# Self-attention transposes copied a step later, and cross-attention steps that begin with the scores

## The reference, cut to what matters

```
# part 1: causal self-attention, 16 heads of 32, gated
proj = layer_norm(x) @ W_in.T + b_in                 # q, k, v, p, y
k = (1 - smear) * k + smear * k_prev
pos = cumsum(sigmoid(y))                             # forget gates
attn = softmax(q k^T / sqrt(32) + causal - relpos)
x = LN(x + LN(silu(p) * (attn @ v) @ W_out.T))
# part 2: cross-attention, 16 heads of 64: queries from x, keys and values
# from 512 rows (256 of the context, masked, and the 256 of x itself)
q = LN(x) @ Wq ; k, v = concat(LN(ctx), LN(x)) @ Wkv
x = LN(x + softmax(q k^T / 8 + mask) v @ Wout)
# part 3: mixture of 8 experts, top 2, width 1024
x = LN(x + sum over the two experts of gate * (gelu(x W1 + b1) W2 + b2))
```

## Time and profile before

| | |
|---|---|
| runs, median | 2735.02 us |
| profiled execution | 2734.17 us, span of its instructions 2732.4 us |
| PE busy | 2407.9 us (88% of the span) |
| DVE, ACT, POOL busy | 1824.2, 1730.1, 924.7 us (67, 63, 34%) |
| mean granted TensorE clock | 0.954 of full speed |

### The profile page before, as it was taken

How to read it: one execution, slowest core, us unless ns; L and a number is a source line. 1 busy time by engine, 2 the same in 40 slices (tenths; PEclk the granted TensorE clock), 3 DMA queues, 4 the chain that set the end, 5 groups by cost and what they waited for, 6 DMA issues and landing times. The chain is left out here.

```text
span 2732.4 us, 60996 instructions
## 1 busy us (share of the span) xinstructions
PE 2407.9 (88%) x17862; PEld 1991.3 (73%) x17862; DVE 1824.2 (67%) x5239; ACT 1730.1 (63%) x4346; POOL 924.7 (34%) x983
## 2 busy tenths in 40 slices
PE   4888888888499999999999999999999469999991
PEld 3666666666377777777777777777776369999991
DVE  5666666667466667666676667666675268888876
ACT  4777787777356566666666666665665256666762
POOL 2434434443423332233322332223321124444434
PEclk9999999999699999999999999999999679999995
DMA  5545445445100000000000000000000157777765
GB/s 122 154 108 123 104 100 123 106 99 118 40 17 17 9 9 16 16 16 1 16 16 16 9 8 16 16 16 9 9 16 9 46 193 232 231 239 234 242 223 192
DMA packets 160229, 224.40 MB, mean 82 GB/s; under 512 B 33872, under 2 KB 127696, under 8 KB 159568
## 3 DMA queue, kind: packets, MB, share of 16 engines
q1 hardware_dynamic: 149040, 201.88, 26.5%
q0 software_dynamic: 9664, 20.53, 2.2%
q10 hardware_dynamic: 1376, 0.54, 0.1%
HBM read 140.15 MB, written 24.01 MB: 60 GB/s over the span
## 5 line engine op out<-in xcount | busy, mean ns | idle before, releaser
L1514 DVE CUSTOM_DVE_ANT_0 x_prob<-x_score,x_mask_add 128x512 f32<-128x512 f32 x512 | 347.9, 682 | 286.7 <-PE x_score L1745 232.0
L1317 ACT ACTIVATE x_prob<-x_prob,x_low 128x512 f32<-128x512 f32 x512 | 366.4, 718 | 190.3 <-DVE x_low L1514 188.0
L1323 ACT COPY x_pt<-x_ptb 128x512 f32<-128x512 f32 x512 | 272.9, 584 | 255.3 <-PE x_ptb L1757 254.7
L1238 POOL TENSOR_TENSOR x_k_lo<-x_whole,x_k_hi 128x512 fp32r<-128x512 f32 x128 | 168.0, 1313 | 413.6 <-ACT x_k_hi L1363 411.2
L1757 PE MATMUL x_ptb<-ident,x_prob 128*128 128x128 f32 x2048 | 267.4, 274 | 2.0 <-PEq L1788 1.8
L1525 DVE TENSOR_SCALAR x_prob<-x_prob,x_rden 128x512 f32<-128x512 f32 x512 | 264.7, 558 | 0.6
L1774 PE MATMUL x_av<-x_pt,x_vx 128*64 128x256 f32 x2048 | 251.0, 387 | 0.8 <-ACT x_pt L1323 0.8
L1757 PEld LDWEIGHTS x_ptb<-ident,x_prob 128*128 128x128 f32 x2048 | 230.4, 141 | 13.8 <-issue 11.1
L484 ACT ACTIVATE prob<-prob,low 128x128 f32<-128x128 f32 (+1 forms) x512 | 229.9, 457 | 5.0 <-DVE low L727 4.8
L1494 DVE COPY x_whole<-x_proj 128x512 f32<-128x512 f32 x192 | 131.0, 688 | 141.7 <-PE x_proj L1678 140.2
L490 ACT COPY pt<-ptb 128x384 f32<-128x384 f32 x258 | 122.4, 474 | 140.5 <-PE ptb L895 140.5
(11 more groups left out here) (274 smaller groups left out, 7283.9 us busy)
## 6 DMA issues: line engine op xcount, KB each, us to landing
w_s<-w SPq DMA_DIRECT2D x156, 512.0 KB, 4.8
k_parts<-k_hi SPq DMA_DIRECT2D x128, 128.0 KB, 2.4
q_parts<-q_hi SPq DMA_DIRECT2D x128, 128.0 KB, 2.4
k_parts<-pos_parts SPq DMA_DIRECT2D x128, 64.0 KB, 2.4
k_parts<-k_lo SPq DMA_DIRECT2D x64, 128.0 KB, 2.4
q_parts<-q_lo SPq DMA_DIRECT2D x64, 128.0 KB, 2.3
w_s<-expert_rows SPq DMA_DIRECT2D x16, 512.0 KB, 4.8
b_s<-b SPq DMA_DIRECT2D x39, 128.0 KB
```

Source lines behind the costliest of these rows:

```text
L1238: pool.tensor_tensor(part_of(n, q_lo, k_lo), whole_of(n), part_of(n, q_hi, k_hi).bitcast(F32), ALU.subtract).then_inc(low_ready.sem, 1)
L1317: nc.scalar.activation(slot, slot, ACT.Exp, bias=low[:, u:u + 1], scale=-1.0, accum_out=den[:, u:u + 1]).then_inc(exp_ready.sem, 1)
L1323: nc.scalar.copy(pt[:, u % PX_RING, :], ptb[u % 2][:, :]).then_inc(pt_taken[u % 2].sem, 1)
L1514: dve.tensor_tensor_reduce(prob[:, u % PROB_RING, :], score[u % 2][:, :], mask_add[:, :], -X_SCALE, 3.0e38, ALU.add, ALU.min, low[:, u:u + ...
```

## The change

In the self-attention a second constant `COPY_LAG = 3` stands beside `LAG = 2`. ScalarE copies the transposes of head i - 3 in step i instead of those of head i - 2, and does so after the parts of the step instead of before them; TensorE still makes the transposes of head i - 2 in step i, and computes the values of a group a step later (steps 3, 7, 11 and 15 instead of 2, 6, 10 and 14). Three dummy transposes are made once before the loop, so that the first copies have something to read.

In the cross-attention TensorE's step begins with the scores of step i + 1, then come the split products, the transposes of step i - 2, the values, and the whole parts. The scores of the next element's first step move from step 17 to step 18. The ring of probabilities has 8 slots instead of 6. ScalarE and VectorE take the projected parts a step later, and some value parts too.

```diff
--- before.py
+++ after.py
@@ -120,7 +120,7 @@
     XT, YP, KP, QP, WO, PP, VP = 0, 1, 2, 4, 6, 8, 10
     LNS = LN_X, LN_OUT, LN_RES = range(3)
     PROB_RING, PT_RING = 4, 2 * EC
-    LAG = 2
+    LAG, COPY_LAG = 2, 3
     with ExitStack() as stack:
         def sb(name, shape, dt=F32):
             return stack.enter_context(nc.sbuf_tensor(name, shape, dt))
@@ -561,8 +561,8 @@
                     tanh_p(b, n)
 
             act.sem_inc(exp_ready.sem, HEADS)
-            for s in pt_taken:
-                act.sem_inc(s.sem, (HEADS - LAG) // 2)
+            for n, s in enumerate(pt_taken):
+                act.sem_inc(s.sem, (HEADS - COPY_LAG + 1 - n) // 2)
             projections(-1)
             steps = {1: [take_xt], 3: [take_y], 4: [lambda b: smear_k(b, 0)], 5: [lambda b: smear_k(b, 1)], 6: [lambda b: high_k(b, 0)],
                      7: [lambda b: high_k(b, 1), lambda b: take_q(b, 0, 0)], 8: [lambda b: take_q(b, 0, 1)], 9: [lambda b: take_q(b, 1, 0)],
@@ -574,15 +574,15 @@
 
                 for i in range(HEADS):
                     exps(b, i)
-                    take_transposed(*unit(b, i - LAG))
                     for part in parts.get(i, ()):
                         part(b)
+                    take_transposed(*unit(b, i - COPY_LAG))
 
             with act.Fori(0, B - 1) as b:
                 one_pass(b, steps)
             one_pass(B - 1, outputs)
-            for i in range(LAG):
-                take_transposed(*unit(B, i - LAG))
+            for i in range(COPY_LAG):
+                take_transposed(*unit(B, i - COPY_LAG))
             for c in range(TC):
                 take_output(c)(B)
 
@@ -815,7 +815,7 @@
         def _(pe):
             pe.wait_ge(consts, N_CONSTS)
             pe.wait_ge(in_weights, N_IN)
-            for s, n in ((score_filled, HEADS), (pt_filled, HEADS - LAG),
+            for s, n in ((score_filled, HEADS), (pt_filled, HEADS - COPY_LAG),
                          (av_done, HPC - 2)):
                 pe.sem_inc(s.sem, n)
             matmul, transpose = nc.tensor.matmul, nc.tensor.transpose
@@ -924,6 +924,9 @@
             for g in range(HPC):
                 ins = matmul(av[g // 2][:, (g % 2) * S:(g % 2 + 1) * S], ident[:], causal[:], start=True, stop=True)
             ins.then_inc(av_done.sem, 1)
+            for i in range(3):
+                ins = transpose(ptb[(HEADS - COPY_LAG) % 2][:, i * P:(i + 1) * P], ident[:], ident[:])
+            ins.then_inc(pt_filled.sem, 1)
             for m in range(EC):
                 transpose(proj[0][:, m * P:(m + 1) * P], bv[:, m:m + 1].broadcast_to([P, P]), ident[:]).then_inc(bias_spread, 1)
             pe.wait_ge(consts_v, N_VCONSTS)
@@ -954,8 +957,8 @@
 
             def group_over(b, i):
 
-                g = (i - EC - LAG) // EC
-                if (i - EC - LAG) % EC == 0:
+                g = (i - EC - COPY_LAG) // EC
+                if (i - EC - COPY_LAG) % EC == 0:
                     values(*((b, g) if g >= 0 else (b - 1, g + HPC)))
 
             scores(0, 0)
@@ -983,7 +986,7 @@
             with pe.Fori(0, B - 1) as b:
                 one_pass(b, split_parts, whole_parts, True)
             one_pass(B - 1, {}, {4: [skips(range(WO))], 9: outputs[:1], 10: outputs[1:], 13: [skips(range(PP, FILLS))]}, False)
-            for i in range(LAG + 1):
+            for i in range(COPY_LAG + 1):
                 if i < LAG:
                     transposes(*unit(B, i - LAG))
                 group_over(B, i)
@@ -1007,7 +1010,7 @@
     WHOLES = 4
     LNS = LN_LAT, LN_CTX, LN_X2 = range(3)
     UNITS = 2 * HEADS
-    PROB_RING = 6
+    PROB_RING = 8
     QUADS = HEADS // 4
     with ExitStack() as stack:
         def sb(name, shape, dt=F32):
@@ -1387,9 +1390,9 @@
                 elif f in V0[0::2]:
                     take_v(-1, f, V0.index(f), 0)
             steps = {}
-            for n, i in enumerate((8, 9, 10, 11, 12, 13, 13, 14, 15, 16, 17, 18)):
+            for n, i in enumerate((9, 10, 11, 12, 13, 13, 14, 15, 16, 17, 18, 19)):
                 steps.setdefault(i, []).append(part(n))
-            for i, more in ((0, v_part(V1, 0, 1)), (2, v_part(V1, 2, 1)), (4, take_context), (5, take_latents), (6, take_x2_t),
+            for i, more in ((0, v_part(V1, 0, 1)), (3, v_part(V1, 2, 1)), (5, take_latents), (5, take_context), (6, take_x2_t),
                             (9, gate_margin), (14, v_part(V0, 0, 0)), (18, v_part(V0, 2, 0))):
                 steps.setdefault(i, []).insert(0, more)
             last = {0: [v_part(V1, 0, 1)], 2: [v_part(V1, 2, 1)], 6: [take_x2_t], 9: [gate_margin]}
@@ -1598,11 +1601,11 @@
                     take_part(-1, KQ.index(f))
                 elif f == V0[1]:
                     take_v(-1, f, 1, 0)
-            steps = {0: [last_values], 1: [v_part(V1, 1, 1), input_stats], 2: [input_normalised], 3: [residual_sum], 4: [v_part(V1, 3, 1), x2_of],
-                     7: [part(0)], 8: [part(1), best_two], 9: [part(2)], 10: [part(3), list_places], 11: [part(4)],
-                     12: [part(5), part(6)], 13: [part(7)], 14: [part(8)], 15: [part(9)], 16: [v_part(V0, 1, 0), part(10), spread_mask],
-                     17: [part(11)]}
-            last = {0: [last_values], 1: [v_part(V1, 1, 1)], 3: [residual_sum], 4: [v_part(V1, 3, 1), x2_of], 8: [best_two], 10: [list_places]}
+            steps = {0: [last_values], 1: [v_part(V1, 1, 1), input_stats], 2: [input_normalised], 3: [residual_sum], 4: [x2_of], 5: [v_part(V1, 3, 1)],
+                     8: [part(0), best_two], 9: [part(1)], 10: [part(2), list_places], 11: [part(3)],
+                     12: [part(4), part(5)], 13: [part(6)], 14: [part(7)], 15: [part(8)], 16: [part(9), v_part(V0, 1, 0)],
+                     17: [part(10), spread_mask], 18: [part(11)]}
+            last = {0: [last_values], 1: [v_part(V1, 1, 1)], 3: [residual_sum], 4: [x2_of], 5: [v_part(V1, 3, 1)], 8: [best_two], 10: [list_places]}
 
             def one_pass(b, parts):
 
@@ -1802,32 +1805,26 @@
                 else:
                     skip(-1, f)
 
-            def last_values_and_context(b):
-                second[3](b)
-                context_transposed(b)
-
-
-            before_ = {1: second[1], 2: second[2], 4: last_values_and_context, 5: latents_transposed, 6: x2_transposed,
-                       8: kq[1], 9: kq[2], 10: kq[3], 11: kq[4], 12: kq[6], 13: kq[7], 14: kq[8], 15: kq[9], 16: kq[10],
-                       17: kq[11], 18: first[3]}
-            after_ = {0: second[0], 1: output, 6: kq[0], 7: logits, 9: prefixes, 11: kq[5], 13: first[0], 15: first[1],
-                      17: first[2]}
+            split_parts = {0: [second[0]], 1: [second[1]], 2: [second[2]], 4: [second[3]], 7: [kq[0]], 8: [kq[1]], 9: [kq[2]],
+                           10: [kq[3]], 11: [kq[4], kq[5]], 12: [kq[6]], 13: [kq[7], first[0]], 14: [kq[8]], 15: [kq[9], first[1]],
+                           16: [kq[10]], 17: [kq[11], first[2]], 18: [first[3]]}
+            whole_parts = {1: [output], 4: [context_transposed, latents_transposed], 5: [x2_transposed], 7: [logits], 9: [prefixes]}
             scores(0, 0)
-            def one_pass(b, before, after):
+            def one_pass(b, split, whole, more):
 
                 for i in range(HEADS + 3):
-                    if i in before:
-                        before[i](b)
+                    if i + 1 < HEADS:
+                        scores(b, i + 1)
+                    elif i == HEADS + 2 and more:
+                        scores(b + 1, 0)
+                    for part in split.get(i, ()):
+                        part(b)
                     if 2 <= i < HEADS + 2:
                         transposes(b, i - 2)
-                    if i + 1 < HEADS:
-                        scores(b, i + 1)
-                    elif i == HEADS + 1 and kq[0] in after.values():
-                        scores(b + 1, 0)
                     if i >= 4 and i % 2 == 0:
                         values(b, (i - 4) // 2)
-                    if i in after:
-                        after[i](b)
+                    for part in whole.get(i, ()):
+                        part(b)
 
             def skips(fills):
 
@@ -1837,10 +1834,10 @@
                 return part
 
             with pe.Fori(0, B - 1) as b:
-                one_pass(b, before_, after_)
-            one_pass(B - 1, {1: second[1], 2: second[2], 4: second[3], 6: x2_transposed},
-                     {0: second[0], 1: output, 5: skips((CT, LT)), 6: skips((KQ[0],)), 7: logits, 8: skips(KQ[1:3]), 9: prefixes,
-                      11: skips(range(PREFIX + 1, FILLS))})
+                one_pass(b, split_parts, whole_parts, True)
+            one_pass(B - 1, {0: [second[0]], 1: [second[1]], 2: [second[2]], 4: [second[3]]},
+                     {1: [output], 4: [skips((CT, LT))], 5: [x2_transposed], 6: [skips((KQ[0],))], 7: [logits], 8: [skips(KQ[1:3])],
+                      9: [prefixes], 11: [skips(range(PREFIX + 1, FILLS))]}, False)
 
 
```

## The result

The changed kernel takes 2770.16 us in the median (2766.55 to 2772.09), the kernel before 2732.94 in the same session. The ratio is 1.0137, with a 95% interval of 1.0118 to 1.0157 (one slow run of the kernel before, 3154.66 us, is not in it): slower by 37 us, where 28 us less was forecast. The profile after splits this into two parts of opposite sign.

What follows compares the result with a forecast made beforehand. Self-attention was taken as bound by waits between engines, cross-attention by TensorE's own work. 2734 - 32 (self-attention) + 6 (cross-attention boundaries) = 2708, rounded to 2706 us; 8 in 10 range 2664 to 2738.

Steps and rivals of the forecast that it cites:

- The walk through one pass: Self-attention: one pass followed from the scores of step 0 to the next, 2.6 us gained, 2.1 taken.
- 2.3 us in step 2: Self-attention: a new wait of 2.3 us for transposes whose bank's copy now stands behind `take_xt` of step 1.
- 0.4 in step 6: Self-attention, steps 4 to 6: the 1.86 us wait for k_t shrinks to about 0.4.
- 1.4 and 1.3 in steps 9 and 10: Self-attention: output projection waits of 2.34 and 0.84 us become some 1.4 and 1.3, gain 0.5.
- the last, for p_tanh: Self-attention, steps 14 and 15: p_tanh follows its exponentials at once, 1.07 us gained, summed as 1.0.
- the deduction of 0.5: Self-attention: uncounted semaphore latencies at three places of the new chain, 0.15 us each, leave 2.1 of 2.6.
- The rival that it would fall once more in a self-attention pass: Clock also falls at steps 1 and 2, 1.6 us a pass, 2730 us; chance 0.20 together with renamed waits.
- that room hides the parts: Cross-attention: spare time on ACT and DVE hides the later parts; without it, 0.5 us a pass lost.
- Zero, between -12 and +10: Cross-attention: change in TensorE's waits in us, forecast as zero, with -12 if all waits are gone.
- The wait at step 4: Cross-attention: scores wait about 1 us for the mask behind VectorE's residual, instead of 0.7 and 0.2 at two places.
- The boundaries: Cross-attention: two more boundaries a pass between scores, values and products on TensorE, 0.4 us a pass, 6 us lost.
- The slower case: Cross-attention rival: VectorE's residual or expert search ends late, products queue behind waiting scores; 3 us a pass, 2751; chance 0.07.

Runs made afterwards that it cites:

- either half of the edit: Self-attention copies behind the parts but of head i - 2 (2676.18 us), or of head i - 3 but ahead of the parts (2667.91 us); cross-attention of the kernel before.
- the run that has one boundary more instead of two: Changed kernel with context, residual sum and step 1 split products earlier, and whole transposes back in steps 4, 5 and 6: 2708.97 us.
- the lag alone: Kernel before with self-attention copies of head i - 3, still ahead of the parts of the step: 2667.91 us, ratio 0.976.

## Why the prediction was wrong

**The self-attention: mechanism right, size short.** 32 us were forecast, 45 measured alone. The walk through one pass named the places: 2.3 us in step 2 (measured 2.28), 0.4 in step 6 (0.42), 1.4 and 1.3 in steps 9 and 10 (1.16 and 1.20). It gave 2.6 us a pass, and I took 0.5 off for latencies; the passes gained 3.0, with or without a fall of the clock (3.01 and 3.13). By the starts of the scores in one pass at a full clock, counted from those of step 1 and read where both kernels have done the same work:

| scores of step | before | after | gained since the row above | forecast |
|---|---|---|---|---|
| 4 | 6.37 | 7.25 | -0.9 | -0.7 |
| 8 | 16.58 | 15.76 | 1.7 | 1.8 |
| 12 | 27.69 | 26.20 | 0.7 | 0.5 |
| 16 (0 of the next pass) | 38.24 | 35.20 | 1.55 | 1.0 |

The mis-sized terms are the last, for p_tanh, and the deduction of 0.5, which nothing in the runs shows. That either half of the edit would have done better I did not see. The walk held part of it, since the wait of 2.3 us comes from the copy standing behind `take_xt`; the larger part is falls of the clock, which the walk did not price for the halves.

**The clock.** The rival that it would fall once more in a self-attention pass did not come (one fall in 12 of the 14 passes after the first, none in 2); a fall came in the cross-attention, where the granted clock had been full from 771 to 2070 us. I had not thought of it there. It cost 1.7 us a pass, 26 us, shown by the run with the context in step 4.

**The cross-attention: this is the step that failed.** The prediction said that ACT and DVE were busy 820 and 873 of 1299 us and that "that room hides the parts". Mean room is not room at a step. `take_context` moved behind a copy that waits for the transposes of its own step, and TensorE's transposes of x2, moved up a step, need the bank it empties. The prediction put the later parts at nothing, or at one copy of 0.5 us a pass without that room, and did not follow this bank. Taking the context early again did not mend it by itself: the wait only moved to the scores, and it shrank when the transposes went back to their places too. The prediction also said of the waits "Zero, between -12 and +10": measured were 4.5 us a pass instead of 1.24, 49 us. The wait at step 4 was named and sized at 1 us (1.45); the one at step 1 was not: VectorE's reciprocal there stands between two masks and waits 0.61 us for exponentials that ScalarE gives late. Over 800 to 2000 us such waits of the reciprocal rose from 6.2 us in 27 places to 59.4 in 52.

**The boundaries.** 6 us were forecast, 0.4 a pass. With the clock full and the waits taken off, the new order takes 0.7 us a pass more than the old, 10 us, and 0.5 to 0.6 in the run that has one boundary more instead of two. The Trainium skill's rule that a change of tiling mode drains the engine (page "TensorEngine Tiling (Array Packing)", section "Key Properties") agrees with this in sign; no run here changes the number of boundaries apart from the waits.

**The sum.** Waits 49, clock 26 and the 10 us that are neither are 85 us, against 84 measured; the forecast had 0, 0 and 6. The slower case had its mechanism half right (scores ahead of products, VectorE late) with a chance of 0.07; it took only the residual and the routing for late, and priced 3 us a pass where 5.6 came.

## What to carry to other kernels

When engines run hand-made lists of steps, moving a part by one step is priced by the one bank or slot it fills or empties, at that step, on both sides; the busy share of the engine did not show it here. Two edits that cure the same wait should be tried one by one, with the clock read beside the time: here the halves gained 56 and 64 us and both together 45, and most of the difference was how often the clock fell and what a fall cost, which the sum of the waits did not show. A wait taken away at a bound engine may come back whole at the next instruction, so it is counted again after each edit.

## What was not expected of the hardware

In a phase where TensorE had run at a full clock for 1300 us, every pass of 92 us of the changed kernel has a stretch of 3.4 us at half the clock (1.2 GHz), behind a new wait of 1.92 us, with others of 1.1 and 1.5 us ahead of it. In the pass shown it runs from 1121.0 to 1124.4 us, after TensorE had resumed at 1119.53. Without that wait, and with the sum of the waits as large as before (1.10, 1.44, 1.48 and 0.43 us), the clock stayed full. The length of one wait does not decide it: with the lag alone TensorE waited 1.85 us for q_hi in each self-attention pass and the clock stayed full, and in the changed kernel passes with the same wait of 2.28 us in step 2 came with a fall (37.72 us) and without one (36.23 us).
